# Routing seven of eight sequences inside the attention that precedes it

## The chip, the cores and the metric

One program on one core of a Trainium2 chip. The metric is device time in microseconds (us) of the whole program, a two-layer transformer forward pass. The kernel before the change took 2766.77 us, the median of three runs (2761.01 to 2768.17). The execution that the profiler recorded took 2773.74 us.

## The reference

The input is 8 sequences of 512 tokens with 256 values each, in float32. Four stages follow each other: attention with 16 heads, a mixture of 8 experts with the best 2 of them for each token, a cosine attention, and a mixture of 64 experts. The change concerns the end of the first stage and the beginning of the second, for which the reference computes, with a layer norm ahead of each and a residual behind it:

```python
att = jax.nn.softmax(jnp.where(causal, att, -jnp.inf), axis=-1)
y = jnp.einsum('bhts,bhsd->bhtd', att, v)
x = x + (y.transpose(0, 2, 1, 3).reshape(b, t, d) @ Wproj.T + bproj)
...
logits = _layernorm(x) @ gate_w
top_w, top_idx = jax.lax.top_k(logits, TOP_K)
```

## The kernel before

Tokens lie on 128 partitions, in 32 tiles of 128 tokens (NT = 32), 4 tiles for a sequence (TB = 4). SBUF keeps all of them in g.x. Products in float32 are made of three products of split values (a high part and a low part).

**attention0_phase** goes through the 8 sequences and, in each, through 8 pairs of heads. Its order is written out by hand: STEP is the list of units of one pair, BETWEEN adds units to some pairs, and ORDER is the list that TensorE, VectorE and ScalarE all follow. In the first sequence's notation, a unit ("b1", 2) is the second part of the scores of pair 2. Below, "pair 7 of a sequence" is the step in which b0, b1 and b2 of that pair run. The matmul outputs of most units (RINGED) go round through three PSUM tiles, a_ring: a unit on TensorE waits until the other engines have taken the output of the unit three places before it (wait_taken). While sequence s runs its pairs, the units x and p0 to p3 make the queries, keys and values of sequence s + 1, and t and y finish the output of sequence s - 1.

GpSimd has one job in this phase, stack: for each of the four tiles of the next sequence it applies the rotary factors and writes the high and low parts into q_stack and k_stack (stack_tile, 13 operations of 128 to 512 values a partition). It starts when VectorE has written qk of a tile (biased, L393), and TensorE needs the last tile at unit ("qk", 0) of the next sequence (L631), which comes in pair 5 of the present one. After that it adds a bias (add_bias, L302).

The SyncE queue fills two DRAM buffers, sorted_x and sorted_y, with zeros in the same phase: 4 MB from SBUF, then copies from DRAM to DRAM of up to 4 MB each (L281).

**route0_phase** begins when attention0_phase has ended on all engines. It goes through 4 groups of two sequences (8 tiles). For each group VectorE computes the norm's statistics (L813 to L822 and rsqrt_seed), GpSimd refines the reciprocal root in 12 small operations (rsqrt_refine, L79 to L85), VectorE normalises (L828), TensorE transposes (L1002), ScalarE and VectorE split the result (L978, L835), TensorE makes the gate's logits (L1014, and L1023 to turn them back), VectorE picks the two experts (choose, 16 operations, L844 to L874), TensorE counts ranks with products of 0 and 1 (find_ranks, L1031 to L1036), and VectorE makes row numbers (place, 8 operations, L879 to L891). GpSimd then scatters the normed tokens into sorted_x: one indirect DMA of 128 rows of 1 KB for each tile and each of the two experts (L792), 64 in all. The phase ends when all of them have landed. Behind the last group VectorE also works out which expert each slot of 256 rows has, SyncE loads the first expert's weights, and VectorE and ScalarE split them (L964, L966, L991). experts0_phase follows.

Of the kernel before, what the change touches and what calls it, by code (L numbers as in the profile page):

```python
# [23 lines left out]
F32 = mybir.dt.float32  # L24
# [64 lines left out]
def attention0_phase(nc, g, t):  # L89

    W3 = 3 * D
    with ExitStack() as ctx:
# [6 lines left out]
        def sig(name, per_turn=0):  # L99
# [21 lines left out]
        straight = sb("straight", [P, 2, H0, DH0])  # L121
# [20 lines left out]

        w_raw = probs[0][:, :, :].rearrange("p j c -> p (j c)")[:, 0:KC * W3].rearrange("p (c n) -> p c n", c=KC)
# [17 lines left out]
                   ("b1", 2): ("t",), ("b2", 2): ("y",), ("a2", 1): ("n",)}  # L161
        ORDER = []
        for step in range(-3, B * PAIRS + 2):
            for what, ahead in STEP:
# [4 lines left out]
                for extra in BETWEEN.get((what, r_), ()):  # L169
                    of = s_ - 1 if extra in ("t", "y") else s_ + 1  # L170
                    if 0 <= of < B:
                        ORDER.append((extra[0], of, int(extra[1:] or 0)))

        RINGED = [unit for unit in ORDER if unit[0] in ("qk", "a0", "a1", "a2", "b0", "b1", "b2", "x", "p", "t", "y")]
# [4 lines left out]
        CLEARED, SPLITS = 11, 11 + 4  # L179

        BATCHES = ((0, TB), (TB, 2 * TB), (2 * TB, NT))
        steps_of = lambda batch: 2 * (batch[1] - batch[0]) + 5
        PREPARED = steps_of(BATCHES[0]) + steps_of(BATCHES[1]) + TB // 2 * 13
# [9 lines left out]
        turn_step, stacked = sig("turn_step", 11 * TB), sig("stacked", 2 * TB)  # L193
# [8 lines left out]
        attT_done, attT_hi, attT_lo = sig("attT_done", KC), sig("attT_hi", KC), sig("attT_lo", KC)  # L202
        proj_done, proj_added = sig("proj_done", TB), sig("proj_added", TB)
# [3 lines left out]
        def stack_tile(engine, n, m, turned, straight, step, done, turn):  # L207

            pairs_of = lambda ap: ap.rearrange("p h (d two) -> p h d two", two=2)
            for q in range(2):  # L210
                for e in range(2):
                    engine.tensor_tensor(pairs_of(turned[:, q])[:, :, :, e], pairs_of(qk[:, n, q])[:, :, :, 1 - e],
                                         pairs_of(unrope[:, n, q:q + 1, :])[:, :, :, e].broadcast_to([P, H0, DH0 // 2]),
                                         ALU.mult).then_inc(step.sem, step.tick())
                engine.tensor_tensor(straight[:, q], qk[:, n, q], rope[:, n, q:q + 1, :].broadcast_to([P, H0, DH0]),
                                     ALU.mult).then_inc(step.sem, step.tick())
            engine.wait_ge(step.sem, step.at(step.n, turn))
            for at in (0, DH0):
                engine.tensor_tensor(q_stack[m][:, n, :, at:at + DH0], straight[:, 0], turned[:, 0],
                                     ALU.add).then_inc(step.sem, step.tick())  # L220
            for at in (0, 2 * DH0):
                engine.tensor_tensor(k_stack[m][:, n, :, at:at + DH0], straight[:, 1], turned[:, 1],
                                     ALU.add).then_inc(step.sem, step.tick())
            engine.tensor_tensor(qk[:, n], straight[:, :], turned[:, :], ALU.add).then_inc(step.sem, step.tick())
# [12 lines left out]
        def _(sp):  # L237
# [21 lines left out]
            for j in range(2):  # L259
                rows = slice(j * HALF, (j + 1) * HALF)  # L260
                for u in range(2):
                    cut = slice(u * HALF, (u + 1) * HALF)
                    sp.dma_start(const_raw[rows, 0, u, :], t["ident"][cut, :]).then_inc(const_loaded.sem, const_loaded.tick(16))
                    for kind in range(2):
                        sp.dma_start(const_raw[rows, 1 + kind, u, :], t["causal"][kind, cut, :]).then_inc(const_loaded.sem,
                                const_loaded.tick(16))
            load_x(2)
# [4 lines left out]
            for at in range(0, TOKENS, step):  # L272
                sp.dma_start(t["sorted_x"][at:at + step, :].rearrange("(n p) d -> p n d", p=P), zeros).then_inc(zeroed.sem,
                        zeroed.tick(16))
            sp.wait_ge(zeroed.sem, zeroed.at(zeroed.n))
            for rows, start in (("sorted_x", TOKENS), ("sorted_y", 0)):
                for at in range(start, BLOCKS * SLOT_TOKENS, TOKENS):
                    size = min(TOKENS, BLOCKS * SLOT_TOKENS - at)
                    dst, src = (t[name][a:a + size, :].rearrange("(p r) d -> p (r d)", p=P)
                                for name, a in ((rows, at), ("sorted_x", 0)))  # L280
                    sp.dma_start(dst, src).then_inc(spread_zeros.sem, spread_zeros.tick(16))  # L281
# [2330 lines left out]
```

## Time and profile before

| what | us |
|---|---|
| median of three runs | 2766.77 |
| the profiled execution | 2773.74 |
| its span, from the first to the last instruction | 2772.1 |
| attention0_phase | 0 to 580 |
| route0_phase | 580 to 717 |
| experts0_phase to the end | 717 to 2772 |
| TensorE busy, share of the span | 87% |
| VectorE / ScalarE / GpSimd busy, share of the span | 66% / 48% / 29% |

The page of the profile names engines PE (TensorE matmul), PEld (its weight loads), DVE (VectorE), ACT (ScalarE), POOL (GpSimd) and SP (SyncE). In its picture of 40 slices of 69.3 us, PE is at 9 tenths or more in most, and falls to 5, 2 and 6 tenths in the slices from 555 to 763 us, with its clock down to 5 to 9 tenths of full speed. A row of a timeline has start, duration, engine, line of the kernel, operation, output and inputs, and a count of merged instructions; in square brackets stands how long the engine was idle before and what released it.

### The profile page before, as it was taken

The numbers are of one execution on the slowest core, as the hardware profiler recorded it, in microseconds if no ns is written. First come the engines' busy times: TensorE is split into PE (matmuls) and PEld (weight loads), VectorE is DVE, ScalarE is ACT, GpSimd is POOL, SyncE is SP. The second block draws the span as 40 slices with busy tenths as digits, with TensorE's granted clock in tenths as the row PEclk, the third lists the DMA queues.
The fourth block names the chain that finished last, engine by engine and source line by source line (L and its number), as shares of the span: only waits on it lengthen the run. The fifth ranks groups of instructions, "written<-read, shape, count | busy, mean of one in ns | idle before, by whom it ended". The sixth has DMA issues, their size and how long they took to land. (4 is left out here: it accounts for less than half of the span.)

```text
span 2772.1 us, 53723 instructions
## 1 busy us (share of the span) xinstructions
PE 2417.6 (87%) x20524; PEld 2154.1 (78%) x20524; DVE 1825.7 (66%) x3239; ACT 1343.4 (48%) x2061; POOL 814.1 (29%) x1194
## 2 busy tenths in 40 slices
PE   4999999952599999926787788879999999999999
PEld 3666666631599999914676677779999999999999
DVE  7666666663488888859999998367454454544544
ACT  1555555621477777623444444434454544545454
POOL 4555666326200000054666765500000000000000
PEclk7899999976799999957889999989999999999999
DMA  9994000002577777648555556044322222222222
GB/s 304 333 335 154 2 2 2 2 15 87 183 239 239 239 233 233 210 133 188 139 146 147 147 148 161 24 149 145 96 85 89 90 88 87 87 88 87 91 77 87
DMA packets 195374, 373.31 MB, mean 135 GB/s; under 512 B 28964, under 2 KB 105960, under 8 KB 194152
## 3 DMA queue, kind: packets, MB, share of 16 engines
q1 hardware_dynamic: 185816, 343.31, 40.4%
q0 software_dynamic: 9360, 27.27, 3.0%
q8 instruction: 134, 2.20, 0.3%
q14 instruction: 64, 0.52, 0.1%
HBM read 336.95 MB, written 100.66 MB: 158 GB/s over the span
## 5 line engine op out<-in xcount | busy, mean ns | idle before, releaser
L2319 DVE TENSOR_TENSOR e_h_lo<-e_h,e_h_hi 128x512 fp32r<-128x512 f32 x320 | 221.9, 693 | 300.7 <-ACT e_h_hi L2395 300.7
L2457 PE MATMUL e_h_ps<-e_yT_hi,e_w_hi 128*128 128x256 f32 x1280 | 362.4, 283 | 3.0 <-ACT e_h L2381 2.2
L2473 PE MATMUL e_y_ps<-e_w_hi,e_h_hi 128*128 128x256 f32 x1280 | 358.8, 280 | 2.4 <-DVE e_h_lo L2319 2.2
L2457 PE MATMUL e_h_ps<-e_yT_lo,e_w_hi 128*128 128x256 f32 x1280 | 358.3, 280 | 0.0
L2457 PE MATMUL e_h_ps<-e_yT_hi,e_w_lo 128*128 128x256 f32 x1280 | 358.1, 280 | 0.0
L2473 PE MATMUL e_y_ps<-e_w_hi,e_h_lo 128*128 128x256 f32 x1280 | 355.4, 278 | 0.0
L2473 PE MATMUL e_y_ps<-e_w_lo,e_h_hi 128*128 128x256 f32 x1280 | 355.2, 277 | 0.0
L2395 ACT ACTIVATE e_h_hi<-e_h 128x512 fp32r<-128x512 f32 x320 | 202.2, 632 | 276.9 <-DVE e_h L2314 220.6
L2381 ACT ACTIVATE e_h<-e_h_ps,e_b 128x512 f32<-128x512 f32 x320 | 218.9, 684 | 174.9 <-PE e_h_ps L2457 152.5
L2314 DVE TENSOR_TENSOR e_h<-e_h,e_spread 128x512 f32<-128x512 f32 x256 | 176.7, 690 | 133.6 <-ACT e_h L2381 132.5
L462 DVE TENSOR_REDUCE a_top<-a_ring 128x2 f32<-128x1024 f32 (+3 forms) x256 | 204.1, 818 | 73.5 <-PE a_ring L651 72.1
L2457 PEld LDWEIGHTS e_h_ps<-e_yT_hi,e_w_hi 128*128 128x128 f32 x1280 | 243.4, 190 | 4.9 <-ACT e_h L2381 2.6
L2473 PEld LDWEIGHTS e_y_ps<-e_w_hi,e_h_hi 128*128 128x128 f32 x1280 | 240.8, 188 | 4.0 <-DVE e_h_lo L2319 3.5
L2457 PEld LDWEIGHTS e_h_ps<-e_yT_lo,e_w_hi 128*128 128x128 f32 x1280 | 241.5, 189 | 0.0
L2457 PEld LDWEIGHTS e_h_ps<-e_yT_hi,e_w_lo 128*128 128x128 f32 x1280 | 241.3, 189 | 0.0
L2473 PEld LDWEIGHTS e_y_ps<-e_w_lo,e_h_hi 128*128 128x128 f32 x1280 | 240.7, 188 | 0.2
L2473 PEld LDWEIGHTS e_y_ps<-e_w_hi,e_h_lo 128*128 128x128 f32 x1280 | 240.3, 188 | 0.0
L79 POOL TENSOR_TENSOR e_by_tile<-e_by_tile 128x4 f32<-128x4 f32 x24 | 8.6, 360 | 746.4 <-DVE e_by_tile L71 745.1
L517 ACT ACTIVATE a_probs<-a_ring 128x1024 f32<-128x1024 f32 (+1 forms) x192 | 168.8, 881 | 97.8 <-PE a_ring L665 96.6
L1290 PE MATMUL e_y_ps<-e_w_hi,e_h_hi 128*128 128x256 f32 x624 | 178.7, 286 | 3.7 <-DVE e_h_lo L1180 3.3
L1276 PE MATMUL e_h_ps<-e_xT_hi,e_w_hi 128*128 128x256 f32 x624 | 173.8, 279 | 1.6 <-DVE e_xT_lo L1173 1.6
L1276 PE MATMUL e_h_ps<-e_xT_hi,e_w_lo 128*128 128x256 f32 x624 | 173.7, 278 | 0.0
(370 smaller groups left out, 6782.4 us busy)
## 6 DMA issues: line engine op xcount, KB each, us to landing
e_w<-in_w SPq DMA_DIRECT2D x78, 1024.0 KB, 5.6
e_spread<-share_store SPq DMA_DIRECT2D x512, 128.0 KB, 2.8
a_keys<-rows_store SPq DMA_DIRECT2D x128, 256.0 KB
a_queries<-rows_store SPq DMA_DIRECT2D x86, 256.0 KB
a_running_hidden<-rows_store SPq DMA_DIRECT2D x42, 256.0 KB
e_xs<-sorted_x SPq DMA_DIRECT2D x39, 256.0 KB, 4.8
sorted_y<-e_ys POOLq DMA_DIRECT2D x39, 256.0 KB, 5.7
e_stage_buf<-in_w_all SPq DMA_DIRECT2D x10, 512.0 KB, 3.9
```

The lines of the kernel that those rows point to most:

```text
L79: pool.tensor_tensor(tmp, guess, guess, ALU.mult).then_inc(step.sem, step.tick())
L462: dve.reduce_max(top[r % 2][:, tb, :], banks(k)[:, :, at:at + (tb + 1) * P], AX.X).then_inc(top_taken.sem, top_taken.tick())
L517: act.activation(probs_of(s, r)[:, :, B_AT[i]:B_AT[i] + B_WIDTH[i]], banks(k)[:, :, 0:B_WIDTH[i]], ACT.Exp).then_inc(probs_ready.sem, prob ...
L1276: last = pe.matmul(h_ps[:, at:at + SLOT_TOKENS], l, r, start=(m == 0), stop=(m == len(ops) - 1))
L1290: last = pe.matmul(y_ps[n][:, 0:D], h_parts[a][:, f, n * P:(n + 1) * P], w2_parts[k][w][:, f, :], start=(f == 0 and m == 0), stop=(f == FC ...
L2314: dve.tensor_tensor(h[:, q % 2, :], h[:, q % 2, :], spread[r % SPREADS][:, :], ALU.mult).then_inc(scaled.sem, scaled.tick())
L2319: dve.tensor_tensor(h_parts[q % 2][1][:, :], h[:, q % 2, :], h_parts[q % 2][0][:, :], ALU.subtract).then_inc(h_lo.sem, h_lo.tick())
L2381: act.activation(h[:, q % 2, :], h_ps[q % 2][:, :], ACT.Silu, bias=b1[:, c:c + 1]).then_inc(h_ready.sem, h_ready.tick())
L2395: act.activation(h_parts[q % 2][0][:, :], h[:, q % 2, :], ACT.Copy).then_inc(h_hi.sem, h_hi.tick())
L2457: last = pe.matmul(h_ps[q % 2][:, cols], l, r, start=(m == 0), stop=(m == len(ops) - 1))
L2473: last = pe.matmul(y_ps[n][:, 0:D], h_parts[q % 2][a][:, n * P:(n + 1) * P], w2[b][:, c, :], start=(q == 0 and m == 0), stop=(q == CH - 1 ...
```

## The change

The norm, gate, ranks and scatter of sequences 0 to 6 are moved into attention0_phase. Sequence q is routed while sequence q + 1 runs: new entries of BETWEEN place statistics (S) in pair 3, the normalisation (N) in pair 5, transposes (U), logits (L) and the first pick (C0) in pair 6, and the second pick (C1), ranks (K) and rows (W) in pair 7. U, L and K take turns in a_ring. GpSimd refines q's reciprocal root after tile 2 of its stack, and scatters behind add_bias. The normed tokens y lie in the space of qk of tiles 2 and 3, so biased of tile 2 waits until the scatter of the sequence that lies there has landed. The logits are now made with tokens on partitions, 24 products of 8 columns a sequence, without the turn back. route0_phase has one group of one sequence (4 tiles) left, and 8 indirect DMAs.

stack_tile has 8 operations instead of 13: queries and keys are treated together and the copies are written twice by one operation. sorted_y now gets the 4 MB of zeros from SBUF, and sorted_x the first DRAM to DRAM copies; the first scatter waits for these (zeros_spread).

```diff
                    ("b1", 2): ("t",), ("b2", 2): ("y",), ("a2", 1): ("n",),
+                   ("b0", 3): ("S",), ("b1", 5): ("N",), ("b0", 6): ("U",), ("b1", 6): ("L",), ("b2", 6): ("C0",),
+                   ("b0", 7): ("C1",), ("b1", 7): ("K",), ("b2", 7): ("W",)}
...
-            for q in range(2):
-                for e in range(2):
-                    engine.tensor_tensor(pairs_of(turned[:, q])[:, :, :, e], ...
-                engine.tensor_tensor(straight[:, q], qk[:, n, q], rope[...], ALU.mult)
+            for e in range(2):
+                engine.tensor_tensor(pairs_of(turned[:, :])[:, :, :, :, e], pairs_of(qk[:, n])[:, :, :, :, 1 - e], ...
             engine.wait_ge(step.sem, step.at(step.n, turn))
-            for at in (0, DH0):
-                engine.tensor_tensor(q_stack[m][:, n, :, at:at + DH0], straight[:, 0], turned[:, 0], ALU.add)
-            for at in (0, 2 * DH0):
-                engine.tensor_tensor(k_stack[m][:, n, :, at:at + DH0], straight[:, 1], turned[:, 1], ALU.add)
-            engine.tensor_tensor(qk[:, n], straight[:, :], turned[:, :], ALU.add)
+            engine.tensor_tensor(qk[:, n], qk[:, n], rope[:, n]..., ALU.mult)
+            engine.wait_ge(step.sem, step.at(step.n, turn))
+            engine.tensor_tensor(q_stack[m][:, n, :, 0:2 * DH0]..., twice(qk[:, n, 0]), twice(turned[:, 0]), ALU.add)
+            engine.tensor_tensor(k_stack[m][:, n, :, 0:4 * DH0]..., twice(qk[:, n, 1]), twice(turned[:, 1]), ALU.add)
+            engine.wait_ge(step.sem, step.at(step.n, turn))
+            engine.tensor_tensor(qk[:, n], qk[:, n], turned[:, :], ALU.add)
...
             for s in range(1, B):
-                stack(s, s % 2, range(TB))
+                for n in range(TB):
+                    stack(s, s % 2, n)
+                    if n == 2 and s >= 2:
+                        refine_rows(s - 2)
                 add_bias(s)
                 if s == 1:
                     refine(2)
+                else:
+                    scatter(s - 2)
+            refine_rows(B - 2)
+            scatter(B - 2)
+            pool.wait_ge(written.sem, written.at(0, B - 1))
...
+            def scatter(q):
+                if q == 0:
+                    pool.wait_ge(zeros_spread.sem, ZERO_SPREADS * 16)
+                for k in range(2):
+                    pool.wait_ge(rows_ready.sem, rows_ready.at(k + 1, q))
+                    for n in range(TB):
+                        pool.indirect_dma_start(out=t["sorted_x"][:, :], ..., in_=y[:, n, :]).then_inc(written.sem, 16)
...
+            def normalise(q):
+                dve.wait_ge(y_refined.sem, y_refined.at(12, q))
+                if q + 2 < B:
+                    dve.wait_ge(stacked.sem, stacked.at(2 * TB, q + 2))
+                if q:
+                    dve.wait_ge(written.sem, written.at(0, q))
...
                 if what == "p":
+                    if r == 2 and s >= 3:
+                        dve.wait_ge(written.sem, written.at(0, s - 2))
                     biased(s, m, r, k)
...
+            def find_logits(q, k):
+                pe.wait_ge(yT_lo.sem, yT_lo.at(KC, q))
+                for n in range(TB):
+                    last = split_product(ring[k][:, n * E0:(n + 1) * E0], ...)
...
-        GROUPS, GT = B // 2, 2 * TB
-        tiles_of = lambda q: range(q * GT, (q + 1) * GT)
+        GROUPS, GT = 1, TB
+        LAST = NT - TB
+        tiles_of = lambda q: range(LAST + q * GT, LAST + (q + 1) * GT)
```

## Rows read from the trace of the kernel before

**Rows 1.** Windows: stretch, length, each engine's busy us (instructions), clock, DMA share, GB/s
```profile
core 0: us, PE busy (x) PEld busy (x) DVE busy (x) ACT busy (x) POOL busy (x), PEclk, DMA share, GB/s
207.00:271.20 64.20, 63.41 (x716) 43.28 (x712) 42.28 (x78) 36.98 (x48) 38.08 (x56) 1.00 0.51 169
...
259.00:265.00 6.00, 5.90 (x80) 4.17 (x78) 4.56 (x10) 4.55 (x7) 0.00 (x0) 1.00 0.01 3
...
580.00:717.00 137.00, 39.76 (x240) 23.69 (x240) 65.94 (x266) 16.06 (x26) 73.56 (x112) 0.60 0.22 79
```

**Rows 2.** Timeline of the route phase, 580 to 717 us
```profile
580.64 0.09 DVE L894 MEMSET r_three_halves<- 128x32 f32 x1 [0.37 <-PEq L92]
...
590.98 2.70 DVE L813 BATCH_NORM_STATS2 r_stats<-x 128x6 f32<-128x256 f32 x8
...
595.14 2.48 DVE L835 TENSOR_TENSOR r_yT_lo<-r_yT_ps,r_yT_hi 128x512 fp32r<-128x512 f32 x4
...
598.56 2.67 DVE L828 TENSOR_SCALAR y<-x,r_mv,r_rstd 128x256 f32<-128x256 f32 x8 [0.94 <-POOL r_rstd L85]
...
615.28 1.17 POOL L792 DMA_INDIRECT sorted_x<-y,row  x1 [6.51 <-DVE row L889]
...
686.26 0.22 DVE L879 TENSOR_TENSOR r_rank<-r_rank_ps,r_head 128x64 f32<-128x64 f32 x1 [8.76 <-remote]
686.51 0.22 DVE L884 TENSOR_TENSOR r_A<-r_rank,r_pick 128x64 f32<-128x64 f32 x1
...
702.94 1.91 ACT L991 ACTIVATE e_w_hi<-e_w 128x2048 fp32r<-128x2048 f32 x1 [14.34 <-DMA e_w<-in_w]
...
708.41 0.96 POOL L792 DMA_INDIRECT sorted_x<-y,row  x1 [0.30 <-issue]
716.63 0.20 DVE L1167 MEMSET scratch<- 128x1 f32 x6 [14.42 <-PEq L712]
```

**Rows 3.** Groups by line and shape, 580 to 717 us: busy, mean ns, idle before
```profile
L792 POOL DMA_INDIRECT sorted_x<-y,row x64 | 63.7, 996 | 33.5 <-issue 18.3 <-DVE row L889 15.2
```

**Rows 4.** Timeline of the attention: last part of the scores of some pairs, one projection
```profile
219.65 0.68 DVE L393 TENSOR_TENSOR a_qk<-a_ring,a_bias_qkv 128x512 f32<-128x512 f32 x1
...
230.00 0.36 PE L535 MATMUL a_ring<-a_wp_hi,a_xnT_hi 128*128 128x256 f32 x1
...
232.81 0.28 PE L535 MATMUL a_ring<-a_wp_hi,a_xnT_lo 128*128 128x256 f32 x1
...
259.58 1.02 ACT L517 ACTIVATE a_probs<-a_ring 128x1024 f32<-128x1024 f32 x1 [0.22 <-PE a_ring L665]
...
264.86 1.02 ACT L517 ACTIVATE a_probs<-a_ring 128x1024 f32<-128x1024 f32 x1 [0.69 <-PE a_ring L665]
```

**Rows 5.** Timeline around one pass of GpSimd's stack, 212 to 277 us
```profile
212.02 1.00 POOL L212 TENSOR_TENSOR a_turned<-a_qk,a_unrope 128x128 f32<-128x128 f32 x2 [26.03 <-DVE a_qk L393]
...
248.21 0.53 PE L631 MATMUL a_ring<-a_ident_r,a_k_stack 128*128 128x128 f32 x4
...
248.23 2.80 POOL L302 TENSOR_TENSOR x<-x,a_bias_proj 128x256 f32<-128x256 f32 x4
...
276.25 1.00 POOL L212 TENSOR_TENSOR a_turned<-a_qk,a_unrope 128x128 f32<-128x128 f32 x2 [25.22 <-DVE a_qk L393]
```

**Rows 6.** Groups by line and shape, 0 to 640 us: GpSimd by size of operation
```profile
L212 POOL TENSOR_TENSOR a_turned<-a_qk,a_unrope 128x128 f32<-128x128 f32 x120 | 60.2, 523 | 182.7 <-DVE a_qk L393 180.9
L215 POOL TENSOR_TENSOR a_straight<-a_qk,a_rope 128x256 f32<-128x256 f32 x60 | 44.2, 736 | 0.0
L224 POOL TENSOR_TENSOR a_qk<-a_straight,a_turned 128x512 f32<-128x512 f32 x30 | 38.6, 1288 | 0.0
```

**Rows 7.** DMA queue 1, 60 to 240 us: packets, MB, share of 16 engines
```profile
q1 hardware_dynamic: 1152, 59.77, 99.1%
```

**Rows 8.** Timeline while indirect DMAs are being issued, 648 to 656 us
```profile
648.11 1.97 PE L1002 MATMUL r_yT_ps<-ident_f,y 128*128 128x128 f32 x16
...
655.99 0.60 ACT L978 ACTIVATE r_yT_hi<-r_yT_ps 128x512 fp32r<-128x512 f32 x1 [4.29 <-remote]
```

More of the change, by code:

```diff
@@ L120, in attention0_phase @@
         turned = sb("turned", [P, 2, H0, DH0])
-        straight = sb("straight", [P, 2, H0, DH0])
         QUAD = 32
@@ L141, in attention0_phase @@
         att = sb("att", [P, TB, H0, DH0])
+        gate_hi, gate_lo = (sb(f"gate_{part}", [P, KC, E0], F32R) for part in ("hi", "lo"))
+        tri, every = sb("tri", [P, P], BF16), sb("every", [P, P], BF16)
+        ids = sb("ids", [P, TB, E0])
+        y_stats, y_mv = sb("y_stats", [P, TB, 6]), sb("y_mv", [P, TB, 2])
+        y_var, y_rstd, y_newton, y_half = (sb(n_, [P, TB]) for n_ in ("y_var", "y_rstd", "y_newton", "y_half"))
+        logits, masked, A, C, rank = (sb(n_, [P, TB, E0]) for n_ in ("logits", "masked", "A", "C", "rank"))
+        pick = [sb(f"pick{k}", [P, TB, E0]) for k in range(2)]
+        first, row_f = sb("first", [P, TB]), sb("row_f", [P, TB])
+        both = sb("both", [P, TB, E0], BF16)
+        y = qk[:, 2:4].rearrange("p n q h d -> p (n q h d)").rearrange("p (n d) -> p n d", d=D)
+        tri_raw = probs[2][:, 1, 0:P]
+        gate_raw = probs[2][:, 1, P:P + KC * E0].rearrange("p (c e) -> p c e", c=KC)
         w_raw = probs[0][:, :, :].rearrange("p j c -> p (j c)")[:, 0:KC * W3].rearrange("p (c n) -> p c n", c=KC)
@@ L311, in prepare @@
                 refine(1)
-                stack(0, 0, range(TB // 2))
+                for n in range(TB // 2):
+                    stack(0, 0, n)
                 pool.wait_ge(stat_step.sem, stat_step.at(PREPARED))
@@ new lines, in place_rows @@
+            def place_rows(q, k):
+                dve.wait_ge(ranked.sem, ranked.at(1, q))
+                dve.tensor_tensor(rank[:, :, :], ring[k][:, 0:TB * E0].rearrange("p (n e) -> p n e", n=TB),
+                                  g.head[:, :].unsqueeze(1).broadcast_to([P, TB, E0]), ALU.add).then_inc(route_step.sem,
+                                          route_step.tick())
+                routed()
+                dve.tensor_tensor(g.head[:, :], g.head[:, :], ring[k][:, TB * E0:(TB + 1) * E0],
+                                  ALU.add).then_inc(rank_taken.sem, rank_taken.tick())
+                for j in range(2):
+                    dve.tensor_tensor(A[:, :, :], rank[:, :, :], pick[j][:, :, :], ALU.mult).then_inc(route_step.sem,
+                            route_step.tick())
+                    routed()
+                    dve.tensor_reduce(row_f[:, :], A[:, :, :], AX.X, ALU.add).then_inc(route_step.sem, route_step.tick())
+                    routed()
+                    dve.tensor_copy(g.row[j][:, q * TB:(q + 1) * TB], row_f[:, :]).then_inc(rows_ready.sem, 1)
+                    dve.wait_ge(rows_ready.sem, rows_ready.at(j + 1, q))
+                dve.wait_ge(rank_taken.sem, rank_taken.at(1, q))
@@ L831, in low_parts @@
             def low_parts(q):
-                for j in range(2):
+                for j in range(GT // TB):
                     for c in range(KC):
@@ L904, in _ @@
                     split.tick())
[L905 removed]
             dve.wait_ge(split.sem, split.at(split.n))
             normalise(0)
[L908 removed]
             low_parts(0)
[L910 to L920 removed]
+            choose(0)
+            place(0)
             dve.tensor_tensor(apart[:, :], best[1][:, :], best[0][:, :], ALU.subtract).then_inc(exp_step.sem, exp_step.tick())
@@ L974, in high_parts @@
                     act.wait_ge(by_expert.sem, by_expert.at(2 * q))
-                for j in range(2):
+                for j in range(GT // TB):
                     for c in range(KC):
@@ L982, in _ @@
                 high_parts(q)
-                for j in range(2):
+                for j in range(GT // TB):
                     act.wait_ge(by_expert.sem, by_expert.at(2 * q + j + 1))
@@ L995, in turn @@
             def turn(q):
-                for j in range(2):
+                for j in range(GT // TB):
                     pe.wait_ge(y_ready.sem, y_ready.at(q * GT + (j + 1) * TB))
```

239 lines of the change are left out of this document (178 added, 61 removed), and 1 row of the table BETWEEN.

## The prediction

> **What bounds the kernel now.** I read the windows by stage first. In the attention one sequence takes a period of 64.2 us, the distance of two starts of GpSimd's pass, 212.02 and 276.25 [rows 5]. In such a period TensorE is busy 63.4 us, VectorE 42.3, ScalarE 37.0 and GpSimd 38.1, with the clock at 1.00 [rows 1]: TensorE sets the pace there. The route phase, 580 to 717, has TensorE busy 39.8 us of 137 at a mean clock of 0.60 [rows 1]. So I took its timeline next. It is a chain ahead of the first scatter, 580.64 to 615.28, then GpSimd's queue of 64 indirect DMAs, whose last is issued at 708.41, and then a wait until all engines leave the phase at 716.63 [rows 2]. An indirect DMA takes 0.996 us and 0.29 us of issue ahead of it (18.3 us by 64), 1.28 in all [rows 3]; 64 of them are 82 us of the 136. The phase is bound by GpSimd's issue, and work is missing on TensorE.
>
> **The change, part by part.**
>
> *Route phase, gain.* What is left is one group of 4 tiles. The time to the first scatter was 34.6 us. Ahead of it stood statistics of other groups, three times the 4.16 us between the starts 590.98 and 595.14, and one normalisation of 8 tiles, 2.67 us [rows 2]. Without them it is 34.6 - 12.5 - 2.7 = 19.4 us; halving the tiles takes more from the rest, but the refinement and the 16 small picks that follow each other keep their length, and some of the removed work lay beside TensorE's. I take 20.5 us. Then 8 scatters are 10.2 us, and from the last one's issue to the end are 716.63 - 709.37 = 7.3 us: 38.0 us. A second chain ends there too: from the ranks (686.26) to the end of the weights' split (702.94 + 1.91) are 18.6 us [rows 2], and ranks at 19.5 give 38.1 + 0.3 for leaving. I take 38.5, and 716.6 - 580.3 = 136.3 before: a gain of 97.8 us. With 3 us more or less in the chain it is 95 to 101.
>
> *End of the attention, loss.* Sequence 6's rows come at the last pair, about 569 us by the old clock, 11 us ahead of the phase's end at 580.3. Eight scatters and their landing are 10.2 + 7.0, so GpSimd leaves at about 586.5: +6 us. It is 4 to 8 us.
>
> *TensorE's new work.* For each of 7 sequences: 8 transposes, at the pace of 16 in 1.97 us [rows 8] 1.0 us; 24 products for the logits; 8 small products for the ranks, 0.3. No row has a product of 8 columns behind a full weight load of this type. The nearest above is a product of 256 columns, (232.81 - 230.00)/24 = 0.117 us [rows 4], so at most 2.8 us; the nearest below the transpose of 128 columns at 0.12 (1.97/16), which is no less, and I allow down to half, 1.4. I take 2.4, near the upper row, since the weight load is the same. Sum 3.7 us a sequence, 26 us in all (19 to 29), all on the path, since TensorE has 0.8 us of idle time in a period.
>
> *VectorE's new work.* Its operations of this kind follow each other at 0.25 us (686.26 to 686.51) [rows 2]. Statistics are 4 x 0.34 and eight small ones, 2.4 us; the normalisation 4 x 0.33 = 1.3; the low parts 1.3; the copy and two picks 16 x 0.25 = 4.0; rows and head 8 x 0.25 = 2.0. That is 11 us a sequence against 22 idle ones. But it is put in lumps. Pair 7 lasts 264.86 - 259.58 = 5.3 us [rows 4], and in the stretch around it VectorE is already busy 4.6 of 6 us [rows 1]. C1 and W add 3.8. So VectorE is behind by 3.8 - 1.4 = 2.4 us there. S in pair 3, which has about the same length, gives 2.4 - 1.4 = 1.0, and N 0.3. TensorE can run ahead by less than one unit, for a_ring has three tiles, so I take the whole 3.7 us a sequence as a stall, 26 us in all. If the long pairs take it up it is 7 (1 us a sequence); if the chain K waits for C1, W for K, is fully exposed it is 42 (6 us).
>
> *GpSimd.* Its tile took (248.23 - 212.02)/4 = 9.05 us. TensorE's transposes of the new stack start at 248.21, as the last tile ends [rows 5]: there is no slack. By size, operations of 128, 256 and 512 values take 0.52, 0.74 and 1.29 us [rows 6]. The new tile has two of 256, four of 512 and two of 256, with one more wait for itself: 8.1 + 0.2 = 8.3 us, 3.0 less for four. The refinement, 12 x 0.28, is 3.4 more. So the pass ends 0.4 us later than it did, and pair 3's delay by S covers that. The scatter of 10.2 us is new ahead of the pass. Rows are there at about 265 (pair 7's last part and 1 us of W), so it ends at 275.3; the pass starts at 276.25 [rows 5]. I cost both at nothing; without that cover, it would be 1 to 3 us a sequence, which the range has.
>
> *The wait of tile 2.* VectorE waits at p2, L393 at 219.65 [rows 4], until the scatter into which y went has landed, and a_top's reductions queue behind it, so TensorE soon stops too. In steady state the scatter is out at 275.3 and down at about 282.3, and p2 comes at 219.65 + 64.2 = 283.9: nothing, with 1.6 us of slack. The first one differs. The zero fill keeps the 16 DMA engines 99.1% busy, in packets of 59.77 MB/1152 = 52 KB [rows 7]. The DMA share of the period is 0.51 [rows 1], so the fill ends at 207 + 0.51 x 64.2 = 240. The first scatter is issued at 201 to 211, and p2 comes at 219.65, or 226 with the delays above. If its small packets get through, the wait is 0; if they come last, 243 - 226 = 17 us. It is once, not seven times. I take 12, nearer the upper end, since no engine has free time before 240.
>
> The Trainium skill ("DMA: Bandwidth & Descriptors", section on queues, rings and completion order) says that each DMA engine goes round its queues a whole packet at a time. If a turn is one of the recorded packets, it is 180 x 16 x 0.991/1152 = 2.5 us [rows 7], and eight scatters would wait for eight turns, 20 us, an estimate that lands them at about 232; by that rule the stall would be 6 us, and the sum 6 us lower. No row shows both kinds of DMA at once.
>
> *Preparation.* Five small constants on VectorE (1 us) against shorter stacks for two tiles (1 us): nothing.
>
> **Sum**, against the profiled execution of 2773.7 us: -97.8 + 6 + 26 + 26 + 12 = -28 us. The profiled one is 7 us above the median; from the median, 2766.8 - 28 = 2739 us. Because VectorE's stalls are the softest term and my sum has no term for small collisions, I put 3 us on top: 2742 us.
>
> **The rivals.**
>
> *A. The scatters hold up TensorE (slower).* In the route phase, 16 transposes start at 648.11 and are out within 1.97 us by their records, but ScalarE gets the second four of them only at 655.99, after 4.29 us of waiting for a release that no record shows, and VectorE the ranks only 8.76 us after its pick; both while indirect DMAs follow each other on GpSimd [rows 2, 8]. It is 1.1 us or so for a transpose. If TensorE's signals come so late during each scatter in the attention, the 10.2 us of seven scatters, and 2.6 behind each, are nearly lost: about 10 us x 7 = 70 us, for 2742 + 65 = 2807 us. It decides from 25/7 = 3.6 us a scatter, where the gain is gone. Against it: TensorE's starts are on time in the records, and the profiler itself may be what delays the signals. Chance 0.2.
>
> *B. The first wait and the stalls are small (faster still).* If the first scatter gets through the zero fill (-12), and the long pairs take up half of VectorE's lumps (26 to 14), it is 2742 - 24 = 2718 us. The two engines' busy times in a period, 63.4 + 3.7 against 42.3 + 11, speak for it. Chance 0.22.
>
> *C. VectorE's chain is on the path.* Every added microsecond of VectorE counts, 11 x 7 = 77 in place of 52 for the two engines, and GpSimd's missing slack costs 1 us a sequence: 2742 + 25 + 7 = 2774, between 2758 and 2780. For it: three rounds between VectorE and TensorE in pair 7. Chance 0.14.
>
> *D. The change does not do what it says.* If the last group of the route phase is held by the weights' chain and not the scatters, the gain is the same within 1 us (both end at 38 us above), so it has no case of its own.
>
> **How the numbers follow.** The forecast case has 0.44, with a range of its own from 2725 to 2758 (the terms' bounds, not all at once). A has 0.2, B 0.22, C 0.14. The range from 2710 to 2800 takes in B, C and A's lower half. A measurement of this kernel can tell about 0.3%, 8.3 us, from no change, so faster is below 2758.5. Faster: 0.43 + 0.22 = 0.65; same, most of C: 0.13; slower 0.22.
>
> **What the profile would show.** The route phase should be about 38 us long, with 8 of L792, and the last two ends (GpSimd's landing, ScalarE's weight split) within 1 us. The period of a sequence should grow from 64.2 to about 71.6 us, with TensorE busy some 67 us of it and idle mostly in pairs 7 and 3 with VectorE as releaser. The third sequence's p2 should show one idle time of VectorE of some 12 us released by the DMA of the scatter, and the later ones none. GpSimd's tile should take 8.3 us. The attention should end with GpSimd's wait, 6 us behind VectorE. A would show as TensorE or those it releases waiting in the 13 us behind pair 7, more than the rest. The prediction is wrong if the period grows by over 10 us, if the wait of tile 2 returns for each sequence, or if the first one lasts past 25 us.

## The result and the profile after

The changed kernel takes 2813.9 us (median of 4 runs, 2807.9 to 2816.3) beside 2766.7 us (2761.0 to 2768.2) for the kernel before: a ratio of 1.0167, with a 95% interval from 1.0154 to 1.018. It is slower, by 47 us, where 25 us less were forecast. Its profiled execution spans 2809.9 us, 37.8 more than that of before (2772.1), and the readings below add up to these 37.8. The two differences are not the same because the profiled execution of before was 7 us above the median of its runs and that of the changed kernel 2.4 us below.

Windows of the changed kernel first: one sequence in the attention, from one start of GpSimd's pass to the next (the answer to the first line of [rows 1]), and the route phase (the answer to its last).

```profile
core 0: us, PE busy (x) PEld busy (x) DVE busy (x) ACT busy (x) POOL busy (x), PEclk, DMA share, GB/s
321.19:403.46 82.27, 77.31 (x756) 52.26 (x756) 50.50 (x121) 38.15 (x51) 45.73 (x56) 0.83 0.04 14
712.40:754.80 42.40, 6.09 (x30) 3.44 (x30) 18.50 (x71) 3.92 (x5) 10.22 (x20) 0.56 0.24 79
```

The second window holds 3.9 us of entering the phase; what is left, 38.6 us, is what was forecast for the route phase (38.5). The attention did not come out so: a period is 82.3 us instead of 64.2, TensorE is busy 77.3 of them instead of 63.4, and its mean clock is 0.83 where it was 1.00. That last column is the finding. The next view cuts the second half of the same period into windows of 4 us (same columns).

```profile
345.00:349.00 4.00, 2.05 (x25) 1.57 (x24) 3.79 (x16) 2.07 (x3) 2.88 (x9) 0.94 0.00 0
349.00:353.00 4.00, 4.00 (x32) 1.82 (x32) 2.64 (x5) 1.62 (x2) 3.37 (x10) 0.50 0.01 4
353.00:357.00 4.00, 4.00 (x44) 2.88 (x44) 1.29 (x2) 1.32 (x2) 3.84 (x4) 0.70 0.00 0
...
365.00:369.00 4.00, 3.54 (x36) 2.12 (x34) 3.19 (x6) 2.42 (x5) 0.00 (x0) 1.00 0.00 0
369.00:373.00 4.00, 4.00 (x48) 3.67 (x45) 1.29 (x2) 2.14 (x3) 0.00 (x0) 0.93 0.00 0
373.00:377.00 4.00, 4.00 (x29) 2.23 (x29) 0.49 (x2) 0.00 (x0) 0.00 (x0) 0.50 0.02 4
377.00:381.00 4.00, 4.00 (x38) 2.08 (x30) 3.24 (x12) 1.59 (x3) 0.00 (x0) 0.50 0.01 2
381.00:385.00 4.00, 4.00 (x40) 3.08 (x40) 2.63 (x10) 2.21 (x4) 0.00 (x0) 0.50 0.00 0
385.00:389.00 4.00, 2.41 (x24) 1.67 (x21) 2.71 (x9) 1.55 (x2) 0.00 (x0) 0.50 0.00 0
389.00:393.00 4.00, 3.36 (x20) 1.12 (x20) 2.78 (x10) 1.02 (x1) 2.00 (x3) 0.51 0.11 36
393.00:397.00 4.00, 4.00 (x52) 3.20 (x52) 1.29 (x2) 2.42 (x3) 3.08 (x4) 1.00 0.28 99
```

The clock falls from 2.4 to 1.2 GHz twice, from 349 on and from 372 to 393. Read the PE column with care: between 373 and 385 it says 4.00 of 4.00, and yet 29 to 40 instructions pass in 4 us, where 48 did from 369 to 373. A busy share cannot show this loss; only the clock and the counts do. What stood at these places, and the two waits that the prediction named, is in the timeline:

```profile
247.55 0.69 DVE L449 TENSOR_TENSOR a_qk<-a_ring,a_bias_qkv 128x512 f32<-128x512 f32 x1 [14.89 <-DMA sorted_x<-a_qk,row]
...
348.80 0.58 PE L850 MATMUL a_ring<-a_kq_T 64*128 64x256 f32 x2 [1.95 <-DVE a_top L621]
...
370.71 0.27 PE L701 MATMUL a_ring<-a_gate_hi,a_xnT_hi 128*128 128x8 f32 x1
...
372.30 0.25 PE L701 MATMUL a_ring<-a_gate_hi,a_xnT_lo 128*128 128x8 f32 x1
...
373.04 0.35 PE L701 MATMUL a_ring<-a_gate_hi,a_xnT_hi 128*128 128x8 f32 x1
...
389.64 0.79 PE L850 MATMUL a_ring<-a_kq_T 64*128 64x512 f32 x2 [2.23 <-DVE head L555]
```

Ahead of the first fall TensorE stood 1.95 us behind the statistics (S, pair 3). Ahead of the second it stood nowhere: from 365.5 on it had no gap, and it ran the 24 narrow logits products (L, pair 6), fifteen of them at a pitch of 0.11 us (370.71 to 372.30) and the rest, after the fall, at 0.21. Then the picks and rows of pair 7 (C1, K, W) stopped it for 2.23 us at the low clock.

The sum of a period: TensorE's idle time went from 0.8 to 5.0 us (+4.2), its busy time from 63.4 to 77.3 (+13.9). The new work, at the full clock, is 1.1 us of transposes, 24 x 0.113 = 2.7 of logits and 0.3 of ranks, 4.1 in all. What is left, 9.8 us, is by subtraction the cost of the lower clock, which holds for about 28 of the 82.3 us (a mean of 0.83).

Over the run: VectorE's last sum of the attention moved from 580.3 to 712.5, by 132.2: 14.9 for the one wait of tile 2, and 117 for seven sequences, 16.8 each on average. Then VectorE waits 3.9 us to enter the route phase, where it waited 0.4 before: +3.5. From its first row in that phase to its first row behind it the route phase has 38.6 us (716.40 to 754.97) instead of 136.0 (580.64 to 716.63): -97.4. The rest of the program is 0.5 shorter. The sum is 37.8.

```profile
708.87 0.96 POOL L353 DMA_INDIRECT sorted_x<-a_qk,row  x1 [0.30 <-issue]
...
716.40 0.09 DVE L1092 MEMSET r_three_halves<- 128x32 f32 x1 [3.91 <-PEq L92]
```

### The profile page after: what moved, and what is told of

It is laid out like the page before. It is cut to its first block and busy times, and to the rows that moved or that the text cites. A ratio compares the mean times of both kernels' runs of the same rounds, so it can differ in the third digit from the quotient of the medians.

```text
span 2809.9 us, 53900 instructions
## 1 busy us (share of the span) xinstructions
PE 2476.3 (88%) x20594; PEld 2196.5 (78%) x20594; DVE 1834.8 (65%) x3349; ACT 1339.7 (48%) x2054; POOL 801.7 (29%) x1092
## 5 line engine op out<-in xcount | busy, mean ns | idle before, releaser
L2660 PE MATMUL e_y_ps<-e_w_hi,e_h_lo 128*128 128x256 f32 x1280 | 355.9, 278 | 0.0
L1477 PE MATMUL e_y_ps<-e_w_hi,e_h_lo 128*128 128x256 f32 x624 | 174.8, 280 | 0.0
```

The costliest lines, as they stand in the source:

```text
L1477: last = pe.matmul(y_ps[n][:, 0:D], h_parts[a][:, f, n * P:(n + 1) * P], w2_parts[k][w][:, f, :], start=(f == 0 and m == 0), stop=(f == FC ...
L2660: last = pe.matmul(y_ps[n][:, 0:D], h_parts[q % 2][a][:, n * P:(n + 1) * P], w2[b][:, c, :], start=(q == 0 and m == 0), stop=(q == CH - 1 ...
```

## The experiments

Sixteen kernels, each timed in 3 or 5 rounds beside the kernel before (2766 to 2769 us). Unless said otherwise a time is compared with the changed kernel's 2813.9. Where a kernel's interval is not given, differences below some 8 us are not clear of the noise.

**e1, the new stack alone.** The kernel before with `stack_tile` of the change. 

> The kernel before with GpSimd's stack of a tile in 8 operations and nothing else. Both theories below say the same: a tile takes 8.6 us instead of 9.05, but TensorE sets the pace (63.4 of 64.2 us), so the period stays at 64 us and the time within 5 us of before, 2762 to 2770. If the stack costs something of its own in the changed kernel (the operations on 512 values at a time), the period would grow here, by the 18 us or a part of them.

Measured 2760.6 us, a ratio of 0.9971 (0.9955 to 0.9987). GpSimd's tile takes 8.6 us (forecast 8.3), a period 63.9. So the new stack costs nothing, and all of the loss is the routing's. How much it gains by itself is less clear than the ratio looks: in the two profiled executions the attention is only 1.1 us shorter, and 7.6 us lie in the route phase, whose code is that of before. There GpSimd waited 15.2 us in four waits for its rows in before [rows 3], and here 6.5 in one:
```profile
POOL sorted_x L791 <- DVE row L888: 6.5, 1, 6.5
```

**e2, no scatters.** A memset of one column stands in the place of each of the 56 scatters, so the rows of seven sequences never reach sorted_x.
```diff
-                        pool.indirect_dma_start(
-                            out=t["sorted_x"][:, :], out_offset=..., in_=y[:, n, :], in_offset=None).then_inc(written.sem, 16)
+                        pool.memset(g.scratch[:, 2 + k * TB + n:3 + k * TB + n], 0.0).then_inc(written.sem, 16)
```


> The changed kernel, with the 56 scatters of sequences 0 to 6 left out (a tiny memset in place of each; their rows never reach the sorted buffer, everything else runs). Clock theory (TensorE's new narrow work and its stalls let its clock fall to 1.2 GHz for 26 of the 82 us of a period) and stall theory (VectorE's lumps alone): the period stays at 81 to 83 us; only the wait for the first scatter (15 us) and the landing at the attention's end (10 us) go, 2785 to 2795. Rival A of the prediction (scatters hold up TensorE's signals): the period falls to about 72 us and the time to some 2725.

2802.5 us, 11 less; I had expected 19 to 29 less. One period of it, and below it one of the changed kernel, same columns as above:
```profile
310.93:395.91 84.98, 80.02 (x756) 54.34 (x756) 50.77 (x121) 38.51 (x51) 38.42 (x57) 0.80 0.01 2
```
```profile
403.46:488.41 84.95, 80.00 (x756) 54.32 (x756) 50.71 (x121) 38.48 (x51) 45.72 (x56) 0.80 0.04 14
```
In both kernels periods of 82 and of 85 us take turns, and the clock is as low. Rival A of the prediction, which was its one way to a slower kernel, falls. What e2 wins is the single wait and the entry into the route phase:
```profile
705.38 0.09 DVE L1090 MEMSET r_three_halves<- 128x32 f32 x1 [0.36 <-PEq L92]
```

**e3 and e4, the logits products.** e3 adds 8 products of 512 columns that nobody reads. e4 exchanges the sides, so that 512 tokens stream past a gate of 8 columns, and turns the result back in a unit M.
```diff
+                    for c in range(KC):
+                        pe.matmul(ring[k][:, S:2 * S], xnT_hi[:, c, n * P:(n + 1) * P], xnT_hi[:, c, :], start=True, stop=True)
...
+                split_product(ring[k][0:E0, 0:S], [((gate_hi[:, c, :], gate_lo[:, c, :]), (xnT_hi[:, c, :], xnT_lo[:, c, :]))
+                                                   for c in range(KC)]).then_inc(lgT_done.sem, lgT_done.tick())
```


> The changed kernel, with 8 products of 128x512 that nobody reads added among the 24 narrow ones of each sequence's logits: 1.8 us more work for TensorE in each sequence. Clock theory: the clock no longer falls in the logits, some 20 us of each period run at 2.4 GHz instead of 1.2, worth 8 to 10 us, so the period shrinks from 82 to about 75 us and the time to about 2765. Stall theory: nothing is won, and the added work costs 7 x 1.8 = 13 us, 2826.

> The changed kernel, with the logits of a sequence as 6 products of 512 columns, the gate being the loaded side, copied by ScalarE and turned back by 4 small transposes in a unit of its own. TensorE's work for it falls from 2.7 to about 1.9 us. Clock theory: 512 columns each keep the clock at 2.4 GHz, the period falls from 82 to 72 to 75 us, the time to 2750 to 2765. Stall theory: only the 0.8 us of work go, 2808.

e3 took 2812.8 us: no gain, but no loss either for 7 x 8 products more, 15 us of work by their records (two of them take 0.55 us), and the clock of its period is 0.90 in place of 0.83. Below its period stand its windows over the logits (372.3 to 377.1) and behind them:
```profile
321.29:403.45 82.16, 75.10 (x764) 50.87 (x764) 50.82 (x121) 38.05 (x51) 45.67 (x57) 0.90 0.04 14
```
```profile
373.00:377.00 4.00, 4.00 (x28) 3.45 (x27) 0.19 (x1) 0.70 (x1) 0.00 (x0) 1.00 0.01 4
...
385.00:389.00 4.00, 1.70 (x24) 1.25 (x24) 2.95 (x11) 0.99 (x2) 0.00 (x0) 0.68 0.00 0
```
With wide products among them the narrow ones no longer lower the clock. It falls some 10 us later, in pair 7, where TensorE waits for VectorE. TensorE is busy 2.2 us less than in the changed kernel in spite of 2.2 us more work, but idle 7.1 us instead of 5.0, and that takes the gain away.

e4 took 2794.8 us, 19 less, where work alone would give 6. Its windows over the logits (369.8 to 371.3) and behind them:
```profile
370.00:374.00 4.00, 4.00 (x46) 1.74 (x44) 1.16 (x4) 2.17 (x4) 0.00 (x0) 1.00 0.00 0
...
378.00:382.00 4.00, 2.50 (x39) 1.79 (x38) 2.92 (x9) 2.34 (x3) 0.00 (x0) 0.94 0.00 0
382.00:386.00 4.00, 1.75 (x16) 0.99 (x20) 3.69 (x16) 0.19 (x1) 1.00 (x1) 0.50 0.00 0
```
The clock stays at 1.00 through the turned logits. It falls 10 us later, where VectorE's picks leave TensorE only 2.5 of 4 us, and a wait of 2.7 us for the rows follows. My 2765 for e3 and 2750 to 2765 for e4 were wrong: with one cause taken away, the clock falls 10 us later, at the stalls of pair 7.

**e5, e6, VectorE's work in small pieces.** One piece behind each score unit from pair 3 on, the refinement on VectorE too; e5 with e4's logits, e6 with the narrow ones.
```diff
-                   ("b0", 3): ("S",), ("b1", 5): ("N",), ("b0", 6): ("U",), ("b1", 6): ("L",), ("b2", 6): ("C0",),
-                   ("b0", 7): ("C1",), ("b1", 7): ("K",), ("b2", 7): ("W",)}
+                   ("b0", 3): ("S0",), ("b1", 3): ("S1",), ("b2", 3): ("S2",), ("b0", 4): ("S3",), ("b1", 4): ("R0",),
+                   ("b2", 4): ("R1",), ("b0", 5): ("R2",), ("b1", 5): ("N0",), ("b2", 5): ("N1",), ("b0", 6): ("U",), ...
```


> The turned logits of e4, and VectorE's new work cut into pieces of at most some 1.4 us, one behind each of TensorE's score units from pair 3 on (statistics in four pieces, both picks in four, the rows a pair later; the norm of the next sequence half a pair earlier; the refinement on VectorE instead of GpSimd, 2.5 us more work there and 3.4 less in GpSimd's pass). If the falls of the clock that are left in e4 come from the stalls behind VectorE's lumps, they go: granted clock 1.00 through a period, a period of 67 to 69 us, and 2767 - 94 (route phase) + 7 x 4 + 15 + 6 = 2722 us or so. If VectorE's work as such is the bound (rival C of the prediction), cutting it up wins nothing: 2790 to 2800.

> The changed kernel with its narrow logits products, and only VectorE's work cut up as in e5. If the narrow products alone let the clock fall (24 of them in 3 us), it still falls in pair 6, but comes back sooner without the stalls of pair 7: a period of 73 to 75 us, 2760 us. If stalls are all that counts, the clock stays up and the time is within 8 us of e5.

2789.7 and 2808.8 us: no clear difference from e4 (both are at 1.009 of before) and from the changed kernel (1.0156 and 1.0167). The first case of each expectation missed by over 45 us; e5's second, 2790 to 2800 if cutting up wins nothing, came out. The narrow products cost 19 us here, as they did between the changed kernel and e4. A reason why cutting up won nothing stands in e5's timeline, VectorE's rows first, GpSimd's below:
```profile
421.75 1.16 DVE L511 TENSOR_SCALAR a_y_var<-a_y_mv 128x4 f32<-128x4 f32 x1
422.94 1.20 DVE L513 TENSOR_SCALAR a_y_half<-a_y_var 128x4 f32<-128x4 f32 x1
...
424.25 1.25 DVE L71 TENSOR_SCALAR a_y_rstd<-a_y_rstd 128x4 int32<-128x4 int32 x1
```
```profile
421.60 1.28 POOL L256 TENSOR_TENSOR a_q_stack<-a_qk,a_turned 128x512 fp32r<-128x512 f32 x1
422.84 1.28 POOL L258 TENSOR_TENSOR a_k_stack<-a_qk,a_turned 128x512 fp32r<-128x512 f32 x1
424.20 1.27 POOL L261 TENSOR_TENSOR a_qk<-a_qk,a_turned 128x512 f32<-128x512 f32 x1
```
An operation on 4 values a partition, 0.17 us elsewhere, takes 1.2 us, and each of the three ends within 0.03 us of one of GpSimd's (422.91 and 422.88, 424.14 and 424.12, 425.50 and 425.47). It waits inside for GpSimd. The Trainium skill ("SBUF — State Buffer", section on the two separate sides) says that VectorE and GpSimd share one pair of ports, which whichever starts first holds for its whole instruction; of VectorE's operations this concerns those in a two-port mode or with two inputs from SBUF. These rows agree, with 1.0 us as the price of one meeting; whether the operations ran in such a mode they do not say. In the changed kernel only the first of these operations meets GpSimd (0.69 us in place of 0.17), for GpSimd then waits for the others; my pieces put them beside its pass, and three of them cost 3 us more than their size. TensorE stood 2.07 us there, and the clock followed (windows, same columns):
```profile
422.00:426.00 4.00, 2.80 (x40) 1.77 (x38) 3.90 (x5) 2.38 (x3) 3.84 (x4) 1.00 0.00 0
426.00:430.00 4.00, 3.13 (x30) 1.40 (x30) 3.79 (x10) 1.04 (x2) 3.73 (x6) 0.69 0.00 0
430.00:434.00 4.00, 4.00 (x36) 3.07 (x34) 3.17 (x11) 1.67 (x3) 0.00 (x0) 0.50 0.00 0
```
That this is the whole reason is not shown: no run moves these three operations alone.

**e7 and e8, the fill of sorted_y behind the first scatter,** in the changed kernel and in e5.
```diff
+                if rows == "sorted_y":
+                    sp.wait_ge(written.sem, written.at(0, 1))
```


> The changed kernel, with the zero fill of sorted_y (40 MB of large packets) issued only when the first scatter has landed. If the first scatter is held up by the fill, VectorE's 15 us of waiting at the third sequence's tile 2 go, and with them the clock lost behind it: 2795 to 2799 us. If the scatter's landing is long for another reason, nothing changes, 2812.

> e5 and e7 together: if their gains add, 15 us below e5, about 2707 us; the fill then ends later, in the attention, where no other transfer needs the engines.

2813.7 and 2788.7 us: nothing won by either, against 15 to 19 us expected of e7 and more of e8. The wait moved. In e7 VectorE no longer waits 14.9 us for the first scatter but 4.2 us for the second (10.3 in e8), and the fill now keeps the DMA engines busy up to 325 us, about when that one lands. Why the 10.7 us by which e7's wait is shorter are not won stays open; the mean clock of its execution is 0.914 beside 0.920. f3 below gives the price of the wait in another kernel.

**e10, one lump by itself,** in the kernel before, 2.70 us of VectorE in pair 3.
```diff
+                if what == "Z":
+                    for n in range(2 * TB):
+                        dve.bn_stats(dump[:, s, n, :], bias_qkv[:, 0:D])
```


> The kernel before, with 8 statistics operations (0.35 us each, 2.8 us in all) of VectorE put in one piece into pair 3 of 7 sequences, their results unused. The price of one lump by itself. By the sum of the prediction, 2.8 - 1.4 = 1.4 us a sequence, 10 us in all, 2777. By the clock theory TensorE then stands still for 1 to 2 us, the clock falls to 1.2 GHz for 6 to 12 us behind it, and each lump costs 4 to 7 us: 2795 to 2815.

2786.6 us, 18 more than before (14 to 29 by the interval of the ratio) and 2.6 a lump: above the 1.4 of the prediction, below my 4 to 7. TensorE stands 1.44 us in one piece at each of three lumps of the seven (241, 306 and 373 us), just what the prediction's way of counting gives, and the clock is the rest (windows at one of the lumps):
```profile
304.00:308.00 4.00, 2.46 (x37) 1.55 (x33) 3.93 (x9) 2.04 (x3) 3.84 (x7) 1.00 0.00 0
308.00:312.00 4.00, 4.00 (x31) 2.03 (x29) 1.88 (x4) 1.62 (x2) 3.92 (x7) 0.57 0.00 0
```
TensorE then has the low clock for 3.4 us, worth 1.7 us of its work. Six of the seven lumps are followed by 3 to 10 us of low clock; the one at 237 us stalls TensorE as long and is followed by a clock of 1.00. Whether a stall is followed by a fall is not decided by the stall alone.

**e9 and e11, a layout by slack.** The turned logits; statistics in three pieces while GpSimd waits for them; y's norm on ScalarE; picks in three pieces; the rows a pair later; the next norm beside the logits; the next stack's first transposes 2.8 us later; the fill of sorted_y in three parts behind three scatters. e11 also moves GpSimd's refinement into its fourth tile.
```diff
+                   ("b0", 3): ("S0",), ("b1", 3): ("S1",), ("b2", 3): ("S2", "S3"), ("b1", 5): ("N0",), ("b2", 5): ("N1",), ("b0", 6): ("U",),
+                   ("b1", 6): ("L",), ("a1", 0): ("n",), ("b2", 6): ("M", "C0"), ("b0", 7): ("C1",), ("b1", 7): ("C2",), ("b2", 7): ("K",),
+                   ("b0", 0): ("W0'",), ("a1", 2): ("W1'",)}
...
+                        sp.wait_ge(written.sem, written.at(0, 1 + 3 * (at // TOKENS - 1) // (ZERO_SPREADS - 1)))
...
+                stack_tile(pool, n, m, turned, turn_step, stacked, s,
+                           (lambda: refine_rows(s - 2)) if n == TB - 1 and s >= 2 else None)
```


> Routing inside the attention laid out by each engine's slack: the turned logits; y's norm on ScalarE (Identity with scale and bias) instead of VectorE; the statistics in three pieces, the picks in three, the next norm beside the logits, the rows a pair later; the refinement on GpSimd as in the changed kernel, with the first transposes of the next stack 2.8 us later in their pair; the fill of sorted_y cut in three, each part issued behind a landed scatter. VectorE then has 27.6 us to do in pairs 3 to 7, where TensorE has 29.5. If VectorE's amount of work in those pairs is what stalls TensorE (and the stalls what lowers its clock), the period falls from e5's 79 us to 69 to 72, no wait of 15 us is left, and the time is 2725 to 2745. If any work between the pairs does the harm wherever it lies, it stays at 2785.

> e9 with GpSimd's refinement moved from ahead of its fourth tile into it, behind the third operation. In e9 GpSimd waited 2.9 us there for VectorE's seed, its fourth tile came late, TensorE stood still for 3.1 us at the next stack's first transposes and its clock fell for 6 us. If that is all that is left, the period falls from 75 to about 69 us and the time from 2761 to 2715 to 2730. If TensorE is then stopped by the next engine behind (VectorE in pairs 6 and 7), a part of it comes back: 2730 to 2745.

e9 took 2761.0 us, a ratio to before of 0.998 (0.9967 to 0.9993), 53 less than the changed kernel, but 16 above the 2745 that I had as upper end. Its trace named the next bound, GpSimd's pass: it waited for VectorE's seed, and 9 us later TensorE stood for its last tile.
```profile
404.78 0.20 POOL L85 TENSOR_TENSOR a_y_newton<-a_y_rstd 128x4 f32<-128x4 f32 x1 [2.91 <-DVE a_y_rstd L71]
```
```profile
416.80 0.75 PE L902 MATMUL a_ring<-a_ident_r,a_k_stack 128*128 128x128 f32 x4 [3.06 <-POOL a_k_stack L270]
```
e11 took 2745.1 us, a ratio of 0.9919 (0.9901 to 0.9936). Two of its periods:
```profile
301.23:376.04 74.81, 70.64 (x743) 47.57 (x742) 50.42 (x118) 40.71 (x56) 45.90 (x58) 0.93 0.58 197
376.04:447.99 71.95, 67.90 (x742) 45.53 (x742) 50.47 (x118) 40.37 (x56) 45.89 (x58) 0.98 0.26 90
```
The second is the period that the prediction had for the change itself, 71.6 us with 67 busy, and it comes about when the clock is at 0.98. At 0.93 it is 3 us longer.

**e12, f1 to f4, one thing of e11 undone at a time.** All compared with e11's 2745.1.

> e11 with the changed kernel's 24 narrow logits products in place of the turned ones: the price of the form alone, where no stall is near. By work alone it is 2.7 - 1.9 = 0.8 us a sequence, 6 us above e11. Clock theory: the clock falls in the logits and stays at 1.2 GHz for 8 us or more, 5 to 8 us a sequence, 35 to 55 us above e11.

e12 (the 24 narrow products again): 2780.1 us, +35, or 5 us a sequence for 0.8 us of work. Its windows over and behind the logits (432.3 to 435.2):
```profile
430.00:434.00 4.00, 4.00 (x50) 3.51 (x48) 2.82 (x7) 2.54 (x3) 0.00 (x0) 1.00 0.02 4
434.00:438.00 4.00, 4.00 (x43) 2.32 (x46) 1.57 (x7) 0.04 (x1) 0.00 (x0) 0.82 0.00 0
438.00:442.00 4.00, 4.00 (x36) 2.44 (x32) 2.57 (x9) 2.67 (x4) 0.00 (x0) 0.50 0.00 0
442.00:446.00 4.00, 4.00 (x34) 3.06 (x32) 2.51 (x9) 2.05 (x2) 0.00 (x0) 0.50 0.01 2
446.00:450.00 4.00, 4.00 (x40) 1.90 (x36) 3.16 (x10) 1.62 (x2) 0.00 (x0) 0.50 0.02 4
```
No idle time of TensorE in 20 us, and the clock at 0.50 for 13 of them: the form of the products does it by itself. The sequence before shows the same, products from 354.2 to 357.0 us and a clock of 0.50 from 358 on. This period is 75.4 us long at a mean clock of 0.91, e11's at the same place 71.95 at 0.98.

> e11 with y's norm back on VectorE, in its two pieces. 1.4 us more for VectorE in pair 5. If VectorE's amount of work in pairs 3 to 7 is a bound, 1.4 to 4 us a sequence, 2755 to 2773; if only the size of a piece matters (each is 0.7 us), within 5 us of e11, 2745.

> e11 with the first transposes of the next stack where the changed kernel has them, 2.8 us earlier in pair 5, so that GpSimd's pass (four tiles of 8.6 us and a refinement of 3.7) has 36 us instead of 39. If GpSimd's pass is the next bound, TensorE stands 2 us there and the clock falls: 3 to 5 us a sequence for six sequences, 2763 to 2775. If the transposes have slack, 2745.

> e11 with the zero fill of sorted_y in one go again, as in the changed kernel. The first scatter then lands behind the fill and VectorE waits for it at the third sequence's tile 2: the price of the first wait, 12 us by the prediction, 15 by the changed kernel's trace plus what the clock loses behind it: 2757 to 2765.

> e11 with the statistics in one piece (2.9 us) in pair 3 and the picks in two pieces (2.4 and 1.1 us) instead of three. The same work in fewer pieces. By the price of a lump in e10 (2.6 us a sequence for 2.7 us of VectorE), 2 to 5 us a sequence, 2760 to 2780; if VectorE's sum is all that counts, 2745.

f1 (y's norm back on VectorE, in two pieces): 2740.9 us, no loss, and at 0.9897 of before (0.9864 to 0.9929) the fastest kernel of the study, though its interval meets e11's. f2 (transposes early): 2757.3, +12, where I had expected 18 to 30. f3 (fill in one go): 2768.5, +23, where I had expected 12 to 20. f4 (fewer, larger pieces): 2772.5, +27, or 3.9 a sequence for the same work, within the 2 to 5 expected. f3's timeline has the wait of the changed kernel back:
```profile
247.53 0.69 DVE L473 TENSOR_TENSOR a_qk<-a_ring,a_bias_qkv 128x512 f32<-128x512 f32 x1 [13.23 <-DMA sorted_x<-a_qk,row]
```

## Why the prediction was wrong

**The route phase** was right: -97.4 us for -97.8 between the two profiled executions. The structure held too. In the changed kernel's timeline the ranks come 19.5 us into the phase (from 716.40; forecast 19.5), and then the chain of the weights ends it, 19.1 us later (forecast 18.6):
```profile
735.89 0.19 DVE L1077 TENSOR_TENSOR r_rank<-r_rank_ps,head 128x32 f32<-128x32 f32 x1 [0.47 <-PE r_rank_ps L1223]
...
748.46 1.23 DVE L1151 CAST e_w_hi<-e_w 128x2048 fp32r<-128x2048 f32 x1 [5.85 <-DMA e_w<-in_w]
```

What was not right is that I took this gain off the median of before. e1 and e10 have the route code of before and need 128.4 and 128.3 us for it, 7.6 less than the profiled execution of before (136.0), which took 7 us more than the median of its runs. So the gain against the median is more likely some 90 us, and the forecast some 8 too low. It stays an inference, since no other execution of before has a profile, and why GpSimd waited longer in that one stays open.

**The end of the attention**, +6: +3.5. VectorE waits 3.9 us for the next phase instead of 0.4. In all kernels with the scatters of which I read this place (the changed one, e3, e4, e5, e9, e11, f1) the route phase begins 7.5 us after the start of the last scatter, 6.6 after its issue ends, for the 7.0 that I had from [rows 2]; without scatters (e2) the wait is 0.4. The mechanism was right. The transfer itself lands after 2.4 us (the median); what the rest of the 6.6 is no row shows.

**TensorE's new work**, 3.7 us a sequence: 4.1 measured. Right. The logits took 2.7 for 2.4.

**VectorE's lumps**, 3.7 us a sequence: TensorE's idle time grew by 4.2. Right in size and in place (pairs 3 and 7), though pair 3 stalled it for 1.95 us, not 1.0. f4 confirms that pieces and not the sum matter: 27 us for the same work cut less finely, while 1.4 us a sequence more of VectorE's work (f1) cost nothing.

**The first wait**, +12: 14.9 us, once, and none later. Right, as is the choice of the upper end. The fill ends at 247 us (not at 240), and VectorE goes on at 247.5: the scatter is held up for the fill's whole rest. Its slowest transfer lands after 28.2 us, where the median of all 56 is 2.4. The estimate by the Trainium skill's rule on packets, a landing after 20 us and a stall of 6, was too low. f3 puts the wait's full price at 23 us in e11's layout, clock included.

**The step that failed** is one that is not in the sum. I read a clock of 1.00 from [rows 1] and carried it over to a kernel in which TensorE has gaps and narrow work. The term that is missing is 9.8 us in the period shown. Over the whole attention it is some 59 us: 132.2, less 14.9 for the wait and 7 x 8.3 for the new work and the idle time. The error in the attention and its end is 66 (70 forecast, 135.7 measured). The row that could have warned me was among those I quoted: the route phase of before, with TensorE busy 40 of 137 us, has a clock of 0.60 [rows 1]. And I had priced the logits at the pitch of a product of 256 columns [rows 4] without asking what else a product of 8 columns changes. e12 shows that part alone, 35 us in e11's layout, 6 of them work; in the changed kernel the same exchange is worth 19 (e4). e10 and f4 show the part of the stalls, 18 and 27 us, but with the standing still itself in it (in e10 7 x 1.44 = 10 us), which my sum had. The parts do not add up one by one, as e3 to e6 show: with one cause gone, the next one keeps the clock down. The prediction's own sign of being wrong, a period that grows by over 10 us, came: it grew by 18.

**The rivals.** A, the scatters, had the right sign and the wrong mechanism (e2). That its 2807 lies near the 2813.9 is luck, and its price was worked out as 70 us but added as 65. B had the wrong sign: neither the wait nor the stalls were small. C, VectorE's whole chain, would have made 2774. VectorE is busy 55.9 us in e5's period and 50.7 in e4's, and e5 is not slower; f1 has more on VectorE than e11 and is not slower either, so VectorE's sum is not the bound. That e11 comes out near the forecast of 2742 is in part luck too: it has no first wait, for which 12 us were forecast. The range's upper end, 2800, lacked 14 us. A's own price lay above it, and no rival changed the pace of TensorE's work that the edit doesn't touch.

**GpSimd at no cost**: right for the tile (8.6 us, no wait of TensorE for it in the changed kernel), but only since the period had grown. At 72 to 75 us the pass is the next bound, as e9 and f2 show.

## What to carry over

Before work is put between the matmuls of a dense stage, ask of each piece what TensorE does meanwhile: here most stalls of 1.4 to 2.2 us, and 24 products of 8 columns, were followed by 3 to 20 us at half the clock, and that costs more than the piece. Let the long side stream (512 tokens past the gate, not the gate past 128 tokens), cut other engines' work into pieces of about a microsecond, as in e11 (how small they must be was not tested), and keep VectorE's small operations away from GpSimd's large ones (seen in e5, not tested alone). And where several causes pull one clock down, taking away one shows little: undo them from the good end, one at a time.

## What was not expected of the hardware

- After an indirect DMA as its last work GpSimd lets the next phase begin 7.5 us after that DMA's start, in all seven kernels read, though the transfer lands sooner.
- 24 products of 128x8 lower TensorE's clock without any idle time: they end at 435.2 us, the clock is 0.50 from 437 to 450, through ordinary work (e12).
- 56 added products of 512 columns cost nothing (2812.8 against 2813.9 us): their work, some 15 us, is won back from the clock (e3, 0.90 against 0.83). The clock is 1.00 through the logits, where it fell to 0.50 without them.
- Stalls of 1.44 us are followed by a fall at six lumps and not at the seventh (e10). What decides it stays open.
- VectorE's operation on 128x4 took 1.16 to 1.25 us in place of 0.17 when it met a GpSimd operation of 128x512 (e5). No run tested this by itself.
- In [rows 8] a release came 4.29 us late from a source that no record shows. No wait in the attention of the changed kernel, whose scatters are issued in the same way, has such a releaser; what it was is still open.
